# A graph attention kernel: seven new waits in front of the gathers of chunks 1 to 7

## The chip, the cores and the metric

The kernel runs on one core of one Trainium2 chip. The metric is the device time of one execution in microseconds (us). A comparison measures both kernels on the same chip.

## What is computed

6250 nodes carry 64 features each (x), and 200,000 edges, sorted by their receiver dst, carry two rows of 64 (edge_attr). Two layers follow each other, each with a residual and a layer norm:

```python
x = layernorm(x + L0(x, edge_attr, src, dst))
x = layernorm(x + L1(x, Wq, Wk, Wv, Wout, [src, dst]))
# L0: q = 0.95 * max(z)[src] * e1 + e0;  z_new = 0.2 z + 0.8 * segsum(q) / segsum(e1), where a node has edges
# L1: 4 heads; s = Q[dst] . K[src] / 8 per edge and head; softmax over the edges of a receiver;
#     out = x + mean over heads of (segsum(alpha * V[src])) @ Wout
```

## The kernel before, in words

Five engines run programs of their own and meet in semaphores: SP issues the plain DMAs, POOL (GpSimd) the gathers, PE (TensorE) multiplies, DVE (VectorE) and ACT (ScalarE) compute. P is 128, D is 64, UG is 13 (groups of four blocks of 128 nodes), S2 is 8, CPP is 4, NCH is 391.

**The edge stage** (0 to about 463 us in the profile) streams the edge rows through SBUF and sums them per receiver on PE. **The node stage** up to about 525 us folds the sums and normalises, 13 groups; POOL's `towards` and `normalise` (L551, L568) belong to it, and SP stores each finished group of x1 to DRAM (L433). When all 13 have landed (`s_x1d`, L579) POOL may begin to gather.

**The U stage** makes U, per node and head the row x1 @ (Wq Wk^T), turned. It has 13 steps. In step u PE turns the group's rows (`turn_nodes`, L1421) and multiplies them by A (`through_A`, L1437, which ends in `s_up`); then ACT copies one half of the two PSUM banks to U (`copy_U`, L287, called on L1172, signals `s_uc`) and DVE the other (L871, signals `s_ud`). ACT also keeps the turned rows of the next step (`keep_turned`, L1164). PE and ACT wait for all 13 `s_uc` and 12 `s_ud` before the attention starts.

**The attention stage** goes over 391 chunks of 512 edges. The edges' sender rows of x1 are gathered by POOL: four indirect DMAs per chunk, each 128 rows of 256 bytes, into one of eight slots of XS (`xs`, L269; the gather loop is L580 to L590, each gather adds 16 to `xg[k]`). The indices come from idx2, loaded by SP for a block of 8 chunks (`lx2`, three buffers). In step m of the pipeline PE turns the rows of chunk m (L1461, after `xg`), weighs the rows of chunk m-4 by its probabilities (L1471, `pv_done`), turns the probabilities of chunk m-3 (L1466) and forms the scores of chunk m-1 (L1513, `s_done`), in this order. DVE takes the maximum of chunk m-2 (L955) and updates the running sums l_st and O (L883, L886, `upd`), and masks. ACT exponentiates chunk m-2 (L1227), copies the turned rows to XT (L1193) and the columns of U to Ubuf (L1187, L1188, `u_done`), and copies turned probabilities (L1237). DVE adds 1 to `u_done` before the stage, 4 to `pv_done` and 2 to `s_done` (L821). So `u_done` is c-1 or more once ACT has done its part for chunk c-3.

The eight slots bound how far POOL may be ahead: before the gathers of chunk c (8 or more) it waits for `pv_done` c-3, which is the weighing of chunk c-8, and between the second and third of the four for `s_done` c-2. The first eight chunks have no such wait. A few chunks reach over more than one window of receivers and take an extra pass (`further_visits`).

**The output stage** scales O, multiplies by Wv and Wout, and normalises.

Of the kernel before, what the change touches and what calls it, by code (L numbers as in the profile page):

```python
# [22 lines left out]
def gnn_resnorm_kernel(nc, x, src, dst, edge, Wq, Wk, Wv, Wout, out):  # L23
# [30 lines left out]
    S2 = 8  # L54
# [11 lines left out]
    UG = -(-NB // 4)  # L66
# [5 lines left out]
    with ctx:  # L72
# [6 lines left out]
        def sem(name):  # L79
            return ctx.enter_context(nc.semaphore(name))  # L80
# [165 lines left out]
        s_eps, s_x1, s_x1d, s_xT, s_xTc, s_up, s_uc, s_ud = (  # L246
            sem(n) for n in ("eps_set", "x1_ready", "x1_stored", "xT_done", "xT_copied", "U_done", "U_copied", "U_copied_dve"))
# [21 lines left out]
        def xs(slot, c):  # L269
            return XS[:, (slot * CPP + c) * D:(slot * CPP + c + 1) * D]  # L270
# [187 lines left out]
        def _(pool):  # L458
# [121 lines left out]
            for c in range(NCH):  # L580
                b, k = c // S2, c % S2
                if k == 0:
                    pool.wait_ge(lx2[b % SB], 16 * (b // SB + 1) + (16 if b == NBL - 1 else 0))
                if c >= S2:
                    pool.wait_ge(pv_done, c - S2 + 5)
                for j in range(CPP):
                    if j == CPP // 2 and c >= S2:
                        pool.wait_ge(s_done, c - S2 + 6)
                    pool.indirect_dma_start(xs(k, j), None, x1_dram,  # L589
                                            bass.IndirectOffsetOnAxis(ap=idx2[b % SB][:, k * CPP + j:k * CPP + j + 1], axis=0)).then_inc(xg[k], 16)  # L590
# [995 lines left out]
```

## Time and profile before

| | us |
|---|---|
| timed runs, median of 3 | 2588.42 |
| lowest and highest | 2585.80, 2590.83 |
| span of the profiled execution | 2997.5 |

No time of its own beside the span is given for the profiled execution. It is one execution, recorded by the hardware profiler, and the timed runs are executions without the recorder. Times in the rows are microseconds from the first instruction; a mean is in nanoseconds where it says so. PE's ends are modelled, the starts are recorded. "Remote" is a wait whose release the profile doesn't attribute to an instruction of this core; "issue" is idle time in which nothing visible was waited for.

### The profile page before, as it was taken

How to read it: one execution, taken by the hardware profiler on the slowest of the kernel's cores; microseconds unless marked ns; L12 is line 12 of the kernel's file. 1: busy time of each engine (PE TensorE's matmuls, PEld its weight loads, DVE VectorE, ACT ScalarE, POOL GpSimd, SP SyncE). 2: the span in 40 equal slices, each digit the busy share in tenths (PEclk: the TensorE clock that was granted, in tenths of full speed). 3: DMA queues.
4: the chain of work that ended last, by engine and by line, in shares of the span. 5: the costliest groups of instructions: out<-in, count | busy, mean ns of one | idle time of the engine just before them, and what ended most of it. 6: DMA issues, size and time to landing. Idle time of an engine off the chain costs nothing.

```text
span 2997.5 us, 65526 instructions
## 1 busy us (share of the span) xinstructions
PE 2424.3 (81%) x18960; PEld 1749.1 (58%) x18961; DVE 1716.4 (57%) x5572; ACT 1313.2 (44%) x3792; POOL 1892.7 (63%) x2370
## 2 busy tenths in 40 slices
PE   4999998477888888887878788888888877778877
PEld 3888887254655555555555555555555555555555
DVE  8999997454545454444444444454544444444447
ACT  5555553443444344443444344443444343434434
POOL 3888887464666666666566566666666555656640
PEclk9999995665555555555555555555555555655558
DMA  6887772111111111111121111211112111112101
GB/s 177 257 255 254 254 252 51 21 31 33 32 38 32 39 38 33 38 32 37 30 38 31 36 35 36 38 32 39 37 33 39 29 36 30 37 29 39 31 18 24
DMA packets 178767, 194.85 MB, mean 65 GB/s; under 512 B 98339, under 2 KB 101235, under 8 KB 176481
## 3 DMA queue, kind: packets, MB, share of 16 engines
q1 hardware_dynamic: 128294, 138.91, 16.5%
q0 software_dynamic: 50048, 51.35, 9.1%
q8 instruction: 136, 2.23, 0.3%
q14 instruction: 289, 2.37, 0.3%
HBM read 184.87 MB, written 5.25 MB: 63 GB/s over the span
## 4 chain that ended last, share of the span: by engine, by line
another core or an unknown queue 30%; DVE 29%; issue 21%; DVEq 10%; PE 7%; ACT 1%; POOL 1%; ACTq 0%; DMA 0%; POOLq 0%; SPq 0%
DVE O L886 5%; DVE rmax L955 5%; DVE nm_old L968 4%; DVE l_st L883 3%; DVEq L982 2%; DVE big L723 2%; DVE cur L971 2%; DVEq L908 2%; DVE XT L877 1%; DVE nm_st L974 1%; DVEq L746 1%; DVEq L886 1%; PE psS L1513 1%; DVEq L904 1%
## 5 line engine op out<-in xcount | busy, mean ns | idle before, releaser
L589 POOL DMA_INDIRECT XS<-x_dram,dst_bs x1564 | 1482.4, 948 | 900.6 <-issue 419.9
L883 DVE SCALAR_TENSOR_TENSOR l_st<-l_st,alpha,rsum 64x1 f32 x782 | 168.2, 215 | 925.0 <-remote 891.3
L1471 PE MATMUL psVX<-XS,PmPT 128*128 128x64 f32 x1568 | 334.4, 385 | 243.6 <-ACT PmPT L1237 243.6
L1513 PE MATMUL psS<-XT,Ubuf 96*128 96x512 f32 x522 | 505.8, 1071 | 17.5 <-issue 6.2
L1471 PEld LDWEIGHTS psVX<-XS,PmPT 128*128 128x128 f32 x1568 | 308.8, 293 | 302.5 <-ACT PmPT L1237 302.2
L1237 ACT COPY PmPT<-psT 128x512 f32<-128x512 f32 x196 | 114.7, 585 | 760.1 <-remote 727.8
L1471 PE MATMUL psM<-XS,dst_bs 128*128 128x64 f32 x1560 | 343.2, 398 | 60.6 <-ACT dst_bs L1237 49.4
L1471 PEld LDWEIGHTS psM<-XS,dst_bs 128*128 128x128 f32 x1560 | 341.6, 321 | 71.0 <-ACT dst_bs L1237 58.3
L955 DVE TENSOR_REDUCE rmax<-psS 128x1 f32<-128x512 f32 x391 | 270.2, 691 | 34.2 <-remote 12.7
L1513 PE MATMUL psS<-dst_bs,Ubuf 96*128 96x512 f32 x260 | 250.3, 1065 | 7.1 <-ACT Ubuf L1188 1.6
L1466 PE MATMUL psT<-ident,dst_bs 128*128 128x128 f32 x780 | 207.6, 419 | 37.1 <-issue 34.2
L1227 ACT ACTIVATE dst_bs<-psS,cur 128x512 f32<-128x512 f32 x195 | 134.0, 687 | 234.0 <-DVE cur L971 216.6
L1461 PEld LDWEIGHTS psVX<-ident,XS 128*128 128x128 f32 x392 | 88.3, 226 | 220.8 <-issue 220.6
L1461 PEld LDWEIGHTS psN<-ident,XS 128*128 128x128 f32 x390 | 87.2, 224 | 216.6 <-issue 216.6
L1466 PE MATMUL psT<-ident,PmPT 128*128 128x128 f32 x784 | 203.7, 413 | 11.1 <-issue 7.1
L1227 ACT ACTIVATE PmPT<-psS,cur 128x512 f32<-128x512 f32 x196 | 134.7, 687 | 176.3 <-issue 99.0
L1237 ACT COPY dst_bs<-psT 128x512 f32<-128x512 f32 x195 | 114.1, 585 | 163.5 <-remote 130.5
L877 DVE TENSOR_SCALAR XT<-big,win_ids 32x512 f32<-32x512 f32 x269 | 129.3, 481 | 76.4 <-issue 76.0
L1466 PEld LDWEIGHTS psT<-ident,PmPT 128*128 128x128 f32 x784 | 162.5, 245 | 14.6 <-issue 8.8
L1466 PEld LDWEIGHTS psT<-ident,dst_bs 128*128 128x128 f32 x780 | 138.9, 216 | 54.5 <-issue 43.5
L1513 PEld LDWEIGHTS psS<-XT,Ubuf 96*128 96x128 f32 x522 | 135.1, 318 | 60.2 <-issue 60.1
L511 POOL TENSOR_TENSOR XS<-XS,zm 128x384 f32<-128x384 f32 x98 | 148.7, 1517 | 27.6 <-DVE zm L754 26.6
(281 smaller groups left out, 4133.2 us busy)
## 6 DMA issues: line engine op xcount, KB each, us to landing
big<-in_edge_attr_2x SPq DMA_DIRECT2D x342, 256.0 KB, 3.3
big<-dst_turned SPq DMA_DIRECT2D x49, 512.0 KB
XS<-x_dram,dst_bs POOLq DMA_INDIRECT x1564
O<-in_edge_attr_2x SPq DMA_DIRECT2D x48, 256.0 KB, 3.4
O<-codes_dram SPq DMA_DIRECT2D x200, 6.0 KB
x_dram<-x SPq DMA_DIRECT2D x12, 128.0 KB, 1.9
out<-big SPq DMA_DIRECT2D x12, 128.0 KB
codes_dram<-O SPq DMA_DIRECT2D x3, 384.0 KB
```

Source lines behind the costliest of these rows:

```text
L511: pool.tensor_tensor(buf[:, :, W:2 * W], buf[:, :, 0:W], zm[k // 2 % 2][:, :].unsqueeze(2).broadcast_to([P, 2 * SJ, W]), ALU.mult).then_in ...
L589: pool.indirect_dma_start(xs(k, j), None, x1_dram, bass.IndirectOffsetOnAxis(ap=idx2[b % SB][:, k * CPP + j:k * CPP + j + 1], axis=0)).the ...
L877: dve.tensor_scalar(t[D:96, :], dst_b[J // S2 % SB][:, J % S2 * CH:(J % S2 + 1) * CH], ids, None, ALU.not_equal).then_inc(s, 1)
L883: dve.scalar_tensor_tensor(out=ls, in0=ls, scalar=al[half], in1=rs[half], op0=ALU.mult, op1=ALU.add)
L886: last = dve.scalar_tensor_tensor(out=o, in0=o, scalar=al[half], in1=ps[half, :], op0=ALU.mult, op1=ALU.add)
L955: dve.tensor_reduce(rmax[:, q:q + 1], psSc[q][:, :], AX_X, ALU.max)
L1227: act.activation(Pms[a][:, :], psSc[a][:, :], ACT.Exp, bias=cur[:, a:a + 1], accum_out=rsum[:, a:a + 1]).then_inc(exp_done, 1)
L1237: act.copy(PTs[a][:, :], psT[:, :]).then_inc(pt_done, 1)
L1461: last = pe.transpose(psXc[b][:, j * P:(j + 1) * P], two, ident[:, :])
L1466: last = pe.transpose(ps[:, j * P:(j + 1) * P], probs[:, j * P:(j + 1) * P], ident[:, :])
L1471: last = pe.matmul(ps, pt[:, j * P:(j + 1) * P], xs(J % S2, j), start=(j == 0), stop=(j == CPP - 1))
L1513: pe.matmul(psSc[1 - a][:, :], Ubuf[1 - a][:, :], XT[(J - 1) % 3][:, :], start=True, stop=True).then_inc(s_done, 1)
```

## The change

In the gather loop POOL waits before the gathers of chunks 1 to 7. For chunk 1 it waits for `s_uc` 13 // 2 = 6, for chunk 2 for `s_uc` 13, for chunks 3 to 7 for `u_done` c-1, ACT's part of chunk c-3. Chunk 0 and the chunks from 8 on are as before.

```diff
                 b, k = c // S2, c % S2
                 if k == 0:
                     pool.wait_ge(lx2[b % SB], 16 * (b // SB + 1) + (16 if b == NBL - 1 else 0))
+                if c in (1, 2):
+                    pool.wait_ge(s_uc, UG * c // 2)
+                elif 2 < c < S2:
+                    pool.wait_ge(u_done, c - 1)
                 if c >= S2:
                     pool.wait_ge(pv_done, c - S2 + 5)
                 for j in range(CPP):
```

## Rows read from the trace of the kernel before

**Rows 1.** The head of the page.
```profile
span 2997.5 us, 65526 instructions
```

**Rows 2.** The page's costliest groups: busy, mean ns | idle before, releaser.
```profile
L589 POOL DMA_INDIRECT XS<-x_dram,dst_bs x1564 | 1482.4, 948 | 900.6 <-issue 419.9
```

**Rows 3.** Timeline of POOL, the first 33 gathers: start, us, instruction [idle before].
```profile
526.73 1.16 POOL L589 DMA_INDIRECT XS<-x_dram,dst_bs  x1 [2.24 <-DMA x_dram<-x]
...
531.95 0.94 POOL L589 DMA_INDIRECT XS<-x_dram,dst_bs  x1 [0.30 <-issue]
...
565.64 0.94 POOL L589 DMA_INDIRECT XS<-x_dram,dst_bs  x1 [0.30 <-issue]
593.72 1.14 POOL L589 DMA_INDIRECT XS<-x_dram,dst_bs  x1 [27.14 <-PE psVX L1471]
```

**Rows 4.** Timeline of ACT in the U stage, its copies to U.
```profile
525.87 1.50 ACT L287 COPY big<-psVX 64x256 f32<-64x256 f32 x4 [1.91 <-PE psM L1437]
...
533.88 1.50 ACT L287 COPY big<-psVX 64x256 f32<-64x256 f32 x4 [0.20 <-PE psM L1437]
...
541.69 1.50 ACT L287 COPY big<-psS 64x256 f32<-64x256 f32 x4 [4.60 <-remote]
...
560.62 1.50 ACT L287 COPY big<-psVX 64x256 f32<-64x256 f32 x4 [14.36 <-remote]
...
571.84 1.50 ACT L287 COPY big<-psS 64x256 f32<-64x256 f32 x4 [4.55 <-remote]
...
581.76 1.08 ACT L290 COPY big<-psVX 64x128 f32<-64x128 f32 x4
```

**Rows 5.** Waits from 526 to 584 us: who for whom, us in total, times, longest.
```profile
DVE big L287 <- remote: 32.8, 3, 17.2
ACT big L287 <- remote: 23.5, 3, 14.4
```

**Rows 6.** Timeline of PE: two steps of the U stage, then the first turned chunks.
```profile
533.73 0.48 PE L1437 MATMUL psS<-PmPT,A 64*128 64x256 f32 x1 [0.29 <-issue]
...
537.14 0.48 PE L1437 MATMUL psVX<-PmPT,A 64*128 64x256 f32 x1 [1.91 <-issue]
...
583.58 0.66 PE L1461 MATMUL psVX<-ident,XS 128*128 128x128 f32 x2 [2.48 <-ACT big L290]
584.03 0.63 PE L1461 MATMUL psN<-ident,XS 128*128 128x128 f32 x2
...
587.30 0.63 PE L1461 MATMUL psVX<-ident,XS 128*128 128x128 f32 x2
```

**Rows 7.** The edge stage: 0 to 400 us by windows, and waits from 50 to 455.
```profile
0.00:400.00 400.00, 334.07 (x9756) 296.69 (x9758) 384.39 (x739) 233.69 (x360) 307.65 (x609) 1.00 0.77 240
...
ACT XS L1117 <- PE psT L1327: 84.6, 49, 2.9
```

**Rows 8.** Waits from 900 to 1300 us.
```profile
DVE l_st L883 <- remote: 170.2, 34, 5.1
ACT PmPT L1237 <- remote: 162.5, 34, 4.9
```

**Rows 9.** Timeline of SP: loads of two successive blocks' indices.
```profile
933.89 0.37 SPq L407 DMA_DIRECT2D dst_bs<-in_src  x1
...
980.51 0.37 SPq L407 DMA_DIRECT2D dst_bs<-in_src  x1
```

**Rows 10.** Windows: 900 to 1300 us; the granted clock is the third last number.
```profile
900.00:1300.00 400.00, 337.38 (x1096) 228.56 (x1097) 195.67 (x760) 169.90 (x555) 259.80 (x275) 0.54 0.18 35
```

**Rows 11.** Timeline of PE: chunks turned while no gather goes out.
```profile
589.29 0.38 PE L1461 MATMUL psN<-ident,XS 128*128 128x128 f32 x2
...
591.75 0.38 PE L1461 MATMUL psVX<-ident,XS 128*128 128x128 f32 x2
...
594.50 0.38 PE L1461 MATMUL psN<-ident,XS 128*128 128x128 f32 x2
```

**Rows 12.** The last gather, and the line of the maxima (first and last start).
```profile
2906.55 0.94 POOL L589 DMA_INDIRECT XS<-x_dram,dst_bs  x1 [0.30 <-issue]
...
L955 DVE TENSOR_REDUCE rmax<-psS x391: 684/691/693, 587.5 to 2935.3; 128x1 f32<-128x512 f32 x196
```

**Rows 13.** Timeline of ACT: its last copy for chunk 0.
```profile
585.07 0.24 ACT L1188 COPY Ubuf<-big 64x64 f32 x1
```

**Rows 14.** The page's DMA issues: KB each, median us to landing.
```profile
x_dram<-x SPq DMA_DIRECT2D x12, 128.0 KB, 1.9
```

## The prediction

> **What bounds the kernel now.** I read the head of the page first: the profiled execution spans 2997.5 us [rows 1], 409.1 us more than the median of the timed runs, 2588.42. That gap matters more here than any row of the stage that is changed, so I keep two sums apart: one in the profiled execution's time, one in a timed run's.
>
> Next the costliest groups: 1564 gathers of 948 ns, with 419.9 us of idle time in front of them that waits for nothing [rows 2]. Between the start of the first and of the thirty-second gather lie 38.91 us in 31 steps [rows 3], so one gather costs POOL 1.255 us, the 0.30 us gap included, and a chunk of four 5.02 us. POOL cannot go faster than that through the 391 chunks.
>
> Then the U stage, on ScalarE's timeline. Its thirteen steps (one copy_U each) start at 525.87; the fifth starts at 533.88, a step per 2.00 us. Then come 541.69, 560.62 and 571.84, and the last, narrow one at 581.76, again (581.76-571.84)/5 = 1.98 us per step [rows 4]. Without the hole the stage would end at 525.87 + 12 x 2.00 + 1.08 = 550.95; it ends at 582.84. **The hole is 31.9 us**, and it ends when the first 32 gathers do (565.64 + 0.94) and what is queued has drained. The list of waits gives it to "remote" in 3 long waits of VectorE and 3 of ScalarE [rows 5], and TensorE's rows say why: the matmuls of the sixth step start at 533.73, but both readers get them at 541.69; those of the seventh start at 537.14 and are read at 560.62 [rows 4, 6]. So TensorE's completions come late, by up to 22 us, while gathers go out. In the edge stage, with plain DMAs at 240 GB/s and more and no gathers, the waits for TensorE average 84.6/49 = 1.7 us and none is remote [rows 7].
>
> In the attention the same thing recurs: over 400 us VectorE waits "remote" 34 times for 170.2 us, ScalarE 34 times for 162.5 [rows 8], about 5 us every second chunk. A block of 8 chunks takes 980.51-933.89 = 46.62 us, 5.83 a chunk [rows 9], at a granted clock of 0.54, between the two levels of 1.2 and 2.4 GHz [rows 10]. Where all gathers are in and none goes out, TensorE turns a chunk every 2.46 to 2.75 us [rows 11].
>
> **Which of this a timed run has.** Tail: from the last gather to the end the profile takes 2997.5-2906.55 = 91 us; at least 62.2 of them follow the last maximum at 2935.3 [rows 1, 12], and three chunk steps of 2.75 stand before it, so 70 to 91. With POOL never idle, a run takes 526.73 + 1563 x 1.255 = 2488.3, plus the tail, 2559 to 2579; the timed median leaves 9 to 30 for launch and end. With the hole of 31.9 us in the U stage, gather 33 starts at 593.72 as in the profile [rows 3], and the floor is 593.72 + 1531 x 1.255 = 2515.1 plus the tail, 2585 to 2606: the timed runs (2585.8 to 2590.8) leave between +3 and -18 us. And a timed attention stage cannot have 5.83 a chunk: (2588.4-551-62)/391 = 5.05 at most. That is POOL's 5.02. In a timed run the gathers thus go out nearly back to back for 1950 us, and TensorE delivers eleven fp32 matmuls (two turned tiles, four probabilities, four weighings, one score) per chunk beneath them. In the hole it delivered about forty in 38 us under the same pitch. The late completions must be mostly absent in a timed run, as if recording caused them. The edge stage may also be quicker when nothing is recorded, which would weaken this; hence the rivals.
>
> The SBUF page of the Trainium skill (SBUF: State Buffer, section "SBUF: two separate sides") states that engine ports and DMA ports are disjoint, so that a transfer and a computing engine don't slow each other. The profiled rows [rows 4, 5] look otherwise. By that rule alone the hole is no contention at the SBUF and the change only delays gathers, the forecast below; by the rows taken at face value it is the first rival.
>
> **The change part by part.** It removes and adds no transfer and no computation. It adds seven waits on POOL's queue, in front of chunks 1 to 7. Their own cost lies within the gap of 0.30 us ahead of a gather; nearest rows: chunk boundaries in the burst, where the gap stays 0.30 [rows 3]. I take 0, bound 0 to 7 x 0.3 = 2 us.
>
> Chunk 0 goes at 526.73 and POOL is through at 531.75. Chunk 1 waits for s_uc 6, the end of the sixth step's copy: 533.88 + 2.0 + 1.5 = 537.4, done 542.4. Chunk 2 waits for s_uc 13, the end of the U stage, 550.95. Chunks 3 to 7 wait for u_done of the chunk three before. ScalarE's copies for chunk 0 end 2.5 us after the stage does (585.31 against 582.84, by the rows of the attention's start, [rows 13]) and chunk 2's gathers alone take 5.02, so that wait is over; chunk c's data land some 2 us after its fourth gather (nearest row: 1.9 us for a store, [rows 14]) and are turned and copied in about 3 more, so u_done of chunk c-3 comes some 5 us ahead of POOL. Price 0; if each cost one step, 5 x 1 us.
>
> Queued behind the waits on POOL are all later gathers, and nothing else until the output stage. So POOL idles (537.4-531.75) + (550.95-542.4) = 14.2 us, and chunk 8's first gather is free to go at 550.95 + 24 x 1.255 = 581.1, where before it was at 565.64 + 1.255 = 566.9. Chunk 8 also waits for chunk 0's weighing. In the trace that comes 593.72-583.58 = 10.1 us after the first turned rows [rows 3, 6], so in a run without the hole at 551.7 + 10.1 = 561.8, before 566.9: no cover. After the change chunk 4 lands at 568 and that weighing follows by 570, ahead of 581.1. SP's loads of ids and of dst wait for upd and move with the chunks; they have tens of us of slack.
>
> Sum for a timed run: **+14.2 us**, 2588.4 + 14.2 = **2602.6**, since a POOL that never idles afterwards gives nothing back. For the profiled execution: hole gone, +581.1-593.7 = -12.6, and -8 if POOL is held to 5.83 a chunk from the start; if TensorE's start counts, up to -19. I expect a span of about 2983 there, shorter, while the timed run is longer.
>
> **The rivals.** (A) The hole is real in timed runs: U stage, chunk 8's gate. Let it be X us. Before, chunk 8 goes at the later of 566.9 and 561.8 + X; after, at 581.1. The gain begins to outweigh the loss at **X = 19.3**; at 31.9 it is 12.6 us: 2575.8. For it: the rows are plain, and the hole ends with the gathers. Against it: the floor above, and 5.05 a chunk.
> (B) The hole is there in part, X from 14 to 24.5, or the engines and not POOL pace a timed attention. In the latter case only the start slips: chunk 2 is turned at 551 + 5 + 2 = 558 where it was 551.7 + (587.30-583.58) = 555.4 [rows 6], about 3 us late: 2591. Against pacing by the engines: 2.46 to 2.75 us a chunk when fed [rows 11]. Either way within 0.2% (5.2 us, about what a measurement of this kernel can tell).
> (C) The change does not do what it says, because the counters are already past: s_uc counts ScalarE's steps from zero, u_done starts at 1, and the gathers start when only the first step is under way. I exclude it: it would need a U stage that is through before 531.75.
>
> **How the numbers follow.** Forecast (slower, 2602.6) 0.57; A and smaller gains 0.28; B 0.15. The likeliest case's own range is 2595 to 2606 (waits and steps priced, or X up to 10). The range over all must reach A: 2574 to 2606. Faster by over 0.2% 0.28, within it 0.15, slower 0.57.
>
> **What would show it.** In the profile after: gathers in groups, four from about 526.7, four from about 537, then from about 551 without a break; U-stage steps at 2.0 us throughout and no "remote" wait there; first turned rows of the attention near 552 instead of 583.58; chunk 8's first gather between 581 and 586; 5.83 a chunk later as before. If the hole stays though the gathers are spread, their burst is not its cause. If the timed run is faster by 8 us or more, the step that fails is "late completions are absent in a timed run". If it is unchanged, POOL was not what paces a timed attention.

## The result and the profile after

The changed kernel takes 2596.48 us in the median of 6 runs (2595.19 to 2602.54), the kernel before beside it 2589.62 (2585.80 to 2592.46). The ratio is 1.0034, 95% interval 1.0024 to 1.0045, or +8.8 us (6.2 to 11.7); the two medians lie 6.9 apart. Here and below a cost in us is the ratio less 1, times the median of the kernel before beside it. The change is a small loss. The prediction said +14.2 and slower.

The profile after spans 2600.8 us, its own time is 2602.54: 1.7 us lie around the span. Its head, its busy times, the chain that ended last by engine and by line, and the group of the gathers (busy, mean ns | idle before):

```profile
span 2600.8 us, 65526 instructions
PE 2078.3 (80%) x18960; PEld 1522.9 (59%) x18961; DVE 1722.9 (66%) x5572; ACT 1312.8 (50%) x3792; POOL 1905.7 (73%) x2370
...
POOL 47%; issue 24%; PE 12%; DVE 8%; DVEq 4%; DMA 4%; ACT 1%; ACTq 0%; POOLq 0%; SPq 0%
POOL XS L593 46%; DMA XS<-x_dram,dst_bs 3%; DVE big L727 2%; PE psS L1517 2%; PE psVX L1475 2%; DVEq L750 1%; PE psM L1475 1%; PE psT L1470 1%; PE psVX L1465 1%; DVEq L773 1%; DVE big L287 1%; DVE PmPT L753 1%; PE psA L1411 1%; PE psS L1411 1%; PE psA L1485 1%
...
L593 POOL DMA_INDIRECT XS<-x_dram,dst_bs x1564 | 1495.4, 956 | 497.5 <-issue 461.7
```

Most of the chain is the gathers' line: 46% of the span is POOL issuing them, and of the 24% "issue" the fixed gaps of 0.30 us in front of them (461.7 us in all, 18% of the span) are the larger part. Nothing is left of the 409 us by which the first profile of the kernel before [rows 1] was longer. Before any of it is put down to the change, that profile needs a second look (next section), since the timed runs moved the other way.

POOL's timeline after, around the new waits, at chunk 8's first gather (580.74), at the only later gap (chunk 31, a further visit), and the last gather:

```profile
528.12 1.16 POOL L593 DMA_INDIRECT XS<-x_dram,dst_bs  x1 [2.24 <-DMA x_dram<-x]
529.59 0.94 POOL L593 DMA_INDIRECT XS<-x_dram,dst_bs  x1 [0.31 <-issue]
...
538.84 0.94 POOL L593 DMA_INDIRECT XS<-x_dram,dst_bs  x1 [5.80 <-ACT big L287]
...
550.60 0.94 POOL L593 DMA_INDIRECT XS<-x_dram,dst_bs  x1 [7.08 <-ACT big L290]
...
555.60 0.94 POOL L593 DMA_INDIRECT XS<-x_dram,dst_bs  x1 [0.30 <-issue]
...
580.74 0.94 POOL L593 DMA_INDIRECT XS<-x_dram,dst_bs  x1 [0.30 <-issue]
...
705.27 0.94 POOL L593 DMA_INDIRECT XS<-x_dram,dst_bs  x1 [6.89 <-PE psS L1517]
...
2517.86 0.94 POOL L593 DMA_INDIRECT XS<-x_dram,dst_bs  x1 [0.31 <-issue]
```

The two waits on the U stage are there, released by ScalarE's copies. Less the fixed gap of 0.30 they are 5.50 and 6.78 us of idle time, 12.3 together. The waits on u_done (chunks 3 to 7) cost nothing: the gap stays 0.30, as at 555.60. From 580.74 to 2517.86 the 1531 steps average 1.265 us.

ScalarE in the U stage after, its copies to U:

```profile
527.26 1.50 ACT L287 COPY big<-psVX 64x256 f32<-64x256 f32 x4 [1.91 <-PE psM L1441]
529.89 1.50 ACT L287 COPY big<-psS 64x256 f32<-64x256 f32 x4 [0.73 <-PE psT L1441]
...
537.07 1.50 ACT L287 COPY big<-psS 64x256 f32<-64x256 f32 x4
538.87 1.50 ACT L287 COPY big<-psVX 64x256 f32<-64x256 f32 x4
...
549.26 1.08 ACT L290 COPY big<-psVX 64x128 f32<-64x128 f32 x4
```

No hole. The first step takes 2.63 us (527.26 to 529.89), those behind it 1.80 and the last 1.53, where the prediction took 2.00 for all of them.

### The profile page after: what moved, and what is told of

Same layout as the page of the kernel before. It is cut to its first block, busy times and chain, and to the rows that moved or that the text cites. A ratio compares the mean times of both kernels' runs of the same rounds, so it can differ in the third digit from the quotient of the medians.

```text
span 2600.8 us, 65526 instructions
## 1 busy us (share of the span) xinstructions
PE 2078.3 (80%) x18960; PEld 1522.9 (59%) x18961; DVE 1722.9 (66%) x5572; ACT 1312.8 (50%) x3792; POOL 1905.7 (73%) x2370
## 4 chain that ended last, share of the span: by engine, by line
POOL 47%; issue 24%; PE 12%; DVE 8%; DVEq 4%; DMA 4%; ACT 1%; ACTq 0%; POOLq 0%; SPq 0%
POOL XS L593 46%; DMA XS<-x_dram,dst_bs 3%; DVE big L727 2%; PE psS L1517 2%; PE psVX L1475 2%; DVEq L750 1%; PE psM L1475 1%; PE psT L1470 1%; PE psVX L1465 1%; DVEq L773 1%; DVE big L287 1%; DVE PmPT L753 1%; PE psA L1411 1%; PE psS L1411 1%; PE psA L1485 1%
## 5 line engine op out<-in xcount | busy, mean ns | idle before, releaser
L593 POOL DMA_INDIRECT XS<-x_dram,dst_bs x1564 | 1495.4, 956 | 497.5 <-issue 461.7
L1517 PE MATMUL psS<-XT,Ubuf 96*128 96x512 f32 x522 | 423.2, 907 | 15.8 <-ACT Ubuf L1192 15.7
L1465 PEld LDWEIGHTS psVX<-ident,XS 128*128 128x128 f32 x392 | 58.4, 185 | 395.7 <-issue 394.7
L1465 PEld LDWEIGHTS psN<-ident,XS 128*128 128x128 f32 x390 | 56.2, 182 | 394.6 <-issue 394.3
L1475 PE MATMUL psVX<-XS,PmPT 128*128 128x64 f32 x1568 | 285.8, 347 | 0.7 <-ACT PmPT L1241 0.7
L1475 PEld LDWEIGHTS psM<-XS,dst_bs 128*128 128x128 f32 x1560 | 282.6, 271 | 1.6 <-ACT dst_bs L1241 1.6
L1475 PE MATMUL psM<-XS,dst_bs 128*128 128x64 f32 x1560 | 282.6, 345 | 0.7 <-ACT dst_bs L1241 0.7
L1465 PE MATMUL psVX<-ident,XS 128*128 128x128 f32 x392 | 110.3, 377 | 169.1 <-DMA XS<-x_dram,dst_bs 165.7
L1465 PE MATMUL psN<-ident,XS 128*128 128x128 f32 x390 | 107.9, 371 | 166.5 <-DMA XS<-x_dram,dst_bs 165.2
L1517 PE MATMUL psS<-dst_bs,Ubuf 96*128 96x512 f32 x260 | 202.2, 872 | 7.1 <-ACT Ubuf L1192 7.1
L1470 PE MATMUL psT<-ident,dst_bs 128*128 128x128 f32 x780 | 171.4, 362 | 3.4 <-ACT dst_bs L1231 3.2
```

Of the source, the lines that this page charges most:

```text
L593: pool.indirect_dma_start(xs(k, j), None, x1_dram, bass.IndirectOffsetOnAxis(ap=idx2[b % SB][:, k * CPP + j:k * CPP + j + 1], axis=0)).the ...
L1465: last = pe.transpose(psXc[b][:, j * P:(j + 1) * P], two, ident[:, :])
L1470: last = pe.transpose(ps[:, j * P:(j + 1) * P], probs[:, j * P:(j + 1) * P], ident[:, :])
L1475: last = pe.matmul(ps, pt[:, j * P:(j + 1) * P], xs(J % S2, j), start=(j == 0), stop=(j == CPP - 1))
L1517: pe.matmul(psSc[1 - a][:, :], Ubuf[1 - a][:, :], XT[(J - 1) % 3][:, :], start=True, stop=True).then_inc(s_done, 1)
```

## The experiments

Ten runs follow, on three chips, each beside runs of the kernel before on its chip.

**The kernel before, profiled again.** No edit.

> The kernel before, unchanged, profiled once more. Theory P (late completions come with the one recorded execution, a timed run has none or few): a second profile of the same kernel can have a span near 2588, a U stage that ends near 551, and chunk 8's first gather at 566.9, POOL idle only there and at a few further visits; then the rest of the change's cost is given back somewhere else. Theory H (a part of the hole is in ordinary executions, X near 10 us): U stage ends near 561, chunk 8's first gather near 572. Theory R (the hole is a property of the kernel whenever it is recorded): span near 2997, 202 gaps over 0.35 us between gathers, as in the first profile.

Measured: 2589.64 us, span 2587.9. Head, chain, POOL's timeline at chunk 8's first gather, ScalarE's at the end of the U stage:

```profile
span 2587.9 us, 65526 instructions
...
POOL 47%; issue 24%; PE 11%; DVE 9%; DVEq 4%; DMA 3%; ACT 1%; ACTq 0%; POOLq 0%; SPq 0%
...
566.06 0.95 POOL L589 DMA_INDIRECT XS<-x_dram,dst_bs  x1 [0.31 <-issue]
567.32 0.95 POOL L589 DMA_INDIRECT XS<-x_dram,dst_bs  x1 [0.30 <-issue]
...
547.52 1.08 ACT L290 COPY big<-psVX 64x128 f32<-64x128 f32 x4
...
L589 POOL DMA_INDIRECT XS<-x_dram,dst_bs x1564: 942/947/1195, 526.8 to 2505.1; - x196
```

(The last line is the view by tile: ns min/median/max, first and last start.) The U stage ends at 547.52 + 1.08 = 548.6, where [rows 4] have 582.84, and the gather that had started at 593.72 [rows 3] starts at 567.32 without waiting: 33 gathers back to back from 526.75. In place of the "remote" waits of [rows 8], 900 to 1300 us has visible ones, and POOL waits for nothing but its fixed gap:

```profile
POOL XS L589 <- issue: 95.2, 312, 0.3
...
ACT dst_bs L1237 <- PE psT L1466: 82.1, 35, 4.5
ACT PmPT L1237 <- PE psT L1466: 73.4, 38, 3.8
DVE l_st L883 <- PE psVX L1471: 67.0, 35, 4.0
```

So the hole the change seems made to remove was in one recorded execution. Theory P (the late completions belong to that execution) holds; theory R (the hole is there whenever the kernel is recorded) falls, and theory H (a part of it in every execution) finds nothing in this profile; the run in which only chunk 1 waits tests it by the timed runs.

**A third profile of the kernel before.** No edit, on another chip.

> The kernel before, profiled a third time, on another chip. If late completions of TensorE come with the kernel, one in three profiles or more should show them again (span near 2997, over 200 gaps between gathers). If the first profile was one disturbed execution, this one is like the second: span 2585 to 2595, U stage without a hole, chunk 8's first gather 40.6 us after the first.

Measured: 2586.28 us, and the head and POOL's timeline:

```profile
span 2584.5 us, 65526 instructions
...
567.20 0.94 POOL L589 DMA_INDIRECT XS<-x_dram,dst_bs  x1 [0.30 <-issue]
```

567.20 against a first gather at 526.73: 40.5 us. Of the twelve profiles of this study one has the late completions. What disturbed that execution stays open.

**Only chunk 1 waits.**

```diff
-                if c in (1, 2):
-                    pool.wait_ge(s_uc, UG * c // 2)
-                elif 2 < c < S2:
-                    pool.wait_ge(u_done, c - 1)
+                if c == 1:
+                    pool.wait_ge(s_uc, 6)
```

> Only chunk 1 waits (s_uc 6); POOL idles once, about 5.5 us, then goes on back to back. Theory P: +5.5 us against the kernel before, the idle time passed on one to one. Theory H: the burst of 28 still goes out under the U stage, so the hole stays and hides the wait: 0 to +1 us.

Measured: ratio 1.0019 (1.0010 to 1.0028), +4.9 us (2.6 to 7.3). POOL's timeline:

```profile
539.07 0.94 POOL L591 DMA_INDIRECT XS<-x_dram,dst_bs  x1 [5.47 <-ACT big L287]
```

5.2 us of idle time cost 4.9. The first number is from the profile (5.47 less 0.30), the second from the timed runs. H said 0 to +1 and is out on them too.

**Chunk 1 waits for the whole U stage.**

```diff
-                if c in (1, 2):
-                    pool.wait_ge(s_uc, UG * c // 2)
+                if c == 1:
+                    pool.wait_ge(s_uc, UG)
```

> Chunk 1 waits for the end of the U stage (s_uc 13) and all later chunks follow it: POOL idles once for 17.5 us (533.0 to 550.6), 5 us more than in the changed kernel. Theory P: 17.3 us more than before if all is passed on, 5 us more than the changed kernel (which measured +6.9). Theory H: about 13 us more than before, since before loses some 4 to 5 us itself. Either way +5 against the changed kernel; if it is less, POOL's start does not pace the attention stage.

Measured: ratio 1.0061 (1.0047 to 1.0074), +15.8 us (12.2 to 19.2), by one gap:

```profile
550.87 0.94 POOL L593 DMA_INDIRECT XS<-x_dram,dst_bs  x1 [17.05 <-ACT big L290]
```

16.75 us of idle time.

**Only the waits on u_done.**

```diff
-                if c in (1, 2):
-                    pool.wait_ge(s_uc, UG * c // 2)
-                elif 2 < c < S2:
+                if 2 < c < S2:
                     pool.wait_ge(u_done, c - 1)
```

> Chunks 1 and 2 go out at once, chunk 3 waits for ScalarE's part of chunk 0 (about 552.9 in the time of the changed kernel's profile): POOL idles 9.8 us instead of 12.3. Theory P: 2.5 us less than the changed kernel, +9.8 at most against before. Theory H: twelve gathers are a burst of 15 us, long enough for a small hole at the end of the U stage: +4 to +7 against before.

Measured: ratio 1.0035 (1.0023 to 1.0047), +9.1 us (6.0 to 12.2):

```profile
552.35 0.94 POOL L591 DMA_INDIRECT XS<-x_dram,dst_bs  x1 [10.39 <-ACT Ubuf L1190]
```

10.1 us of idle time. Twelve gathers went out back to back, and the U stage's steps are 1.80 us from the third on all the same. The intervals overlap that of the changed kernel, so "2.5 us less" is not shown. It also shows that the waits on u_done are free only because chunk 2's wait stands in front of them.

**The changed kernel again.** No edit.

> The changed kernel, unchanged, on another chip than the first time, beside the same runs of the kernel before as the next three. Theory P (POOL's idle time is passed on one to one): its profile idles 12.3 us, so about +12 us. If it is again +7 to +9, part of the idle time is given back, and more than in the kernels with one gap.

Measured: ratio 1.0054 (1.0040 to 1.0068), +14.0 us (10.3 to 17.6). The same two gaps:

```profile
529.08 1.16 POOL L593 DMA_INDIRECT XS<-x_dram,dst_bs  x1 [2.24 <-DMA x_dram<-x]
...
539.82 0.94 POOL L593 DMA_INDIRECT XS<-x_dram,dst_bs  x1 [5.83 <-ACT big L287]
...
551.60 0.94 POOL L593 DMA_INDIRECT XS<-x_dram,dst_bs  x1 [7.09 <-ACT big L290]
```

12.3 us again. One comparison gave 8.8, the other 14.0, and the idle time lies between them, just above the first interval and inside the second. That a part is given back is not shown. Profile against profile nothing is given back: the first profile of the changed kernel is 12.9 us longer than the second of the kernel before, 1.4 of them ahead of the first gather, 11.4 from the first gather to the last and 0.1 behind it. That profiled execution was also the slowest of the six (2602.54); where the other five were quicker no profile shows.

**The attention starts late, the gathers don't.** The kernel before with extra copies in the last 5 steps of the U stage, then in all 13 (`UG - 13` for `UG - 5`). They write to places that are unused there.

```diff
                 act.wait_ge(s_up, u + 1)
+                if u >= UG - 5:
+                    for t in ((PmX[:, :], dst_bs[:, 0:CH].bitcast(F32)), (Pms[1], PTs[1]))[u % 2]:
+                        act.copy(t, u_banks[u % 2][0][:, :])
                 copy_U(act.copy, u, 0).then_inc(s_uc, 1)
```

> The kernel before; ScalarE makes two extra copies of 128x512 (0.585 us each) to unused places in each of the last 5 steps of the U stage, so the attention starts some 5.9 us late while all gathers go out as before. By the second profile of the kernel before, TensorE's weighings and scores are 5.6 to 8.6 us ahead of the gathers that wait for them. Theory P: 0 to +1 us. Theory S (the start of the attention paces the end): +5.9.

> The same extra copies in all 13 steps, some 15.2 us. Theory P: only what exceeds the lead of 5.6 us counts, +9.6, and it shows as idle time of POOL at chunks 8 to 13. Theory S: +15.2.

Measured for 5 steps: ratio 1.0005 (0.9996 to 1.0014), +1.3 us (-1.0 to 3.6); from its first gather (526.54) to the end of the U stage it took 26.6 us, 4.8 more than the 21.8 of the second profile of before. For 13 steps: 1.0026 (1.0016 to 1.0037), +6.7 us (4.1 to 9.6), with the U stage 12.1 us longer (529.06 to 562.98), less than the 15.2 I had reckoned. POOL's timeline in the second, at chunks 8, 9 and 12 (chunks 10 and 11 have a gap of 0.58 each):

```profile
573.87 1.13 POOL L589 DMA_INDIRECT XS<-x_dram,dst_bs  x1 [4.74 <-PE psVX L1474]
...
581.87 0.94 POOL L589 DMA_INDIRECT XS<-x_dram,dst_bs  x1 [0.57 <-PE psS L1516]
...
598.38 1.18 POOL L589 DMA_INDIRECT XS<-x_dram,dst_bs  x1 [0.81 <-PE psS L1516]
```

An attention that starts 4.8 us late costs nothing that can be told from zero, 12.1 us late it costs about the idle time that it makes on POOL: 4.44 us at chunk 8 and 1.34 at chunks 9 to 12, 5.8 together. Theory S (the start of the attention paces the end: +5.9 and +15.2, or 4.8 and 12.1 by the stretches measured) falls. The weighing that chunk 8 waits for thus has a lead of 12.1 - 4.44, about 8 us. It covers an attention that starts late. Waits in front of the gathers themselves, which is what the change adds, it does not cover.

**The idle time in the middle.**

```diff
-                    pool.wait_ge(pv_done, c - S2 + 5)
+                    pool.wait_ge(pv_done, c if c in (100, 200, 300) else c - S2 + 5)
```

> The kernel before; only chunks 100, 200 and 300 wait for a later weighing (pv_done c instead of c-3), so that POOL stands still three times some 4 to 7 us in the middle of the stage, and the U stage is untouched. Theory P: the time grows by the sum of these gaps, 12 to 20 us, as at the start. If gaps in the middle cost less than their length, something else paces the stage there.

Measured: ratio 1.0078 (1.0064 to 1.0092), +20.2 us (16.6 to 23.8). The three gaps:

```profile
1042.26 0.94 POOL L589 DMA_INDIRECT XS<-x_dram,dst_bs  x1 [4.22 <-PE psM L1471]
...
1549.66 0.94 POOL L589 DMA_INDIRECT XS<-x_dram,dst_bs  x1 [3.62 <-PE psM L1471]
...
2060.42 0.94 POOL L589 DMA_INDIRECT XS<-x_dram,dst_bs  x1 [8.31 <-PE psM L1471]
```

15.25 us in the one profile. No less than the idle time is lost, so POOL paces the middle of the stage as well. The profiled execution itself took 2603.20, 15.7 us above the median before and close to its own 15.25; three of the other four took 2607.73 to 2610.49. The gaps differ from 3.6 to 8.3 us, and whether those executions had longer ones, or something adds to them, is open.

**A shorter node stage, to gain on both kernels.** The kernel before, where ScalarE's Square also sums (one activation of 64 columns per block) and VectorE's reduction goes.

```diff
-                    act.activation(sq1[(g - 2) % 2][:, 0:nb * D], x1[:, b0 * D:(b0 + nb) * D], ACT.Square).then_inc(g_sq, 1)
+                    for b in range(nb):
+                        last = act.activation(sq1[(g - 2) % 2][:, b * D:(b + 1) * D], x1[:, (b0 + b) * D:(b0 + b + 1) * D], ACT.Square,
+                                              accum_out=stat[:, b0 + b:b0 + b + 1])
+                    last.then_inc(g_sq, 1)
...
-                dve.tensor_reduce(s_, sq1[g % 2][:, 0:nb * D].rearrange("p (b d) -> p b d", d=D), AX_X, ALU.add).then_inc(g_var, 1)
```

> The kernel before with a shorter stage ahead of the first gather: in the node stage ScalarE sums the squares itself (one activation with its sum per block) and VectorE's reduction of them (0.41 us in each of 13 steps of 3.95 us that VectorE fills) is left out. Theory P (POOL never idles after its first gather): what the first gather comes earlier is gained at the end, one to one, some 4 to 5 us: the first gather near 522 and the time 0.2% lower. If the node stage doesn't get shorter, POOL (3.3 us a step) or ScalarE (about 3.0) sets it and nothing changes. If the gather comes earlier and the time stays, theory P is wrong about the start.

Measured: ratio 1.0004 (0.9995 to 1.0013), no change. POOL's first gather, and TensorE's folding of the sums in the same profile:

```profile
526.53 1.16 POOL L589 DMA_INDIRECT XS<-x_dram,dst_bs  x1 [2.23 <-DMA x_dram<-x]
...
474.66 0.77 PE L1402 MATMUL psA<-ident,big 128*128 128x128 f32 x2
...
475.65 0.77 PE L1402 MATMUL psA<-ident,big 128*128 128x128 f32 x2
```

And the windows of 475 to 515 us, first of the kernel before (second profile), then of this one. Busy us stand in the order TensorE, its weight loads, VectorE, ScalarE, POOL, and the granted clock is the third last number:

```profile
475.00:515.00 40.00, 40.00 (x244) 40.00 (x245) 36.24 (x68) 13.62 (x40) 31.01 (x58) 0.50 0.14 31
...
475.00:515.00 40.00, 40.00 (x244) 40.00 (x244) 33.45 (x59) 19.49 (x104) 30.87 (x59) 0.50 0.14 32
```

The gather does not come earlier. TensorE folds a block every 0.985 us without a gap, 3.94 us for a group of four, and is busy for 40.00 of 40 us in both kernels, at a granted clock of 0.50 (the level of 1.2 GHz). The step of 3.95 us is TensorE's; VectorE, at 36.24 us nearly as long, only looked like its owner, and what the edit took from it (2.8 us) changed nothing. Since the first gather did not move, this says nothing about theory P. No kernel here beats the one before.

## Why the prediction was right, and where not

Idle time of POOL that a kernel adds (from its profile, less 0.30 per gap) and what it costs in timed runs:

| kernel | first gather at, us | idle, us | cost, us (95% interval) |
|---|---|---|---|
| attention late, 5 steps | 526.5 | 0 | 1.3 (-1.0 to 3.6) |
| attention late, 13 steps | 529.1 | 5.8 | 6.7 (4.1 to 9.6) |
| chunk 1 only | 528.7 | 5.2 | 4.9 (2.6 to 7.3) |
| u_done only | 527.0 | 10.1 | 9.1 (6.0 to 12.2) |
| the change, two comparisons | 528.1, 529.1 | 12.3 | 8.8 (6.2 to 11.7), 14.0 (10.3 to 17.6) |
| in the middle | 528.7 | 15.25 | 20.2 (16.6 to 23.8) |
| all after the U stage | 528.9 | 16.75 | 15.8 (12.2 to 19.2) |

The kernel before has its first gather at 526.73 to 526.75 in its three profiles. Further visits (chunk 31) are left out of the idle time: that one gap is 4.6 to 6.9 us long in the eleven undisturbed profiles, which alone makes two profiles differ by up to 2.3 us.

- **"A POOL that never idles afterwards gives nothing back"**: right within what the runs can tell. The cost follows the idle time within the intervals, but for two that miss it by 0.6 and 1.4 us. One thing runs beside it: in six of the profiles, none of them of the kernel before, the first gather comes 1.4 to 2.4 us later. The delay begins in the edge stage, which no edit touches (the same matmuls start at 461.90 in the second profile of before and at 463.32 in the first of after). If the timed runs have it too, the cost in the middle is inside its interval and that of the first comparison of the change further outside. Whether it belongs to those kernels or to chance was not tried.
- **+14.2 us of idle time**: the mechanism was right, the size was off by 1.9; it is 12.3. The mis-sized term is the step of the U stage. The 2.00 us were a mean over the first four steps, and these hold the long first one (2.32) and a disturbed fourth (2.10); the two between took 1.80 in that profile too:

```profile
528.19 1.50 ACT L287 COPY big<-psS 64x256 f32<-64x256 f32 x4 [0.42 <-PE psT L1437]
529.98 1.50 ACT L287 COPY big<-psVX 64x256 f32<-64x256 f32 x4
531.78 1.50 ACT L287 COPY big<-psS 64x256 f32<-64x256 f32 x4
```

  From the first copy to the last the profile after has 22.0 us (527.26 to 549.26) where the prediction had 24.0, and the second wait is 6.78 us in place of 8.55. The forecast of 2602.6 us lies 6.1 above the measured 2596.48. The 1.9 us explain a part; the distance from 12.3 us of idle time to a cost of 8.8 no run explains, and the repetition gave 14.0.
- **Chunk 8 free at 566.9 before and 581.1 after**: 567.32 and 580.74 in the profiles. The second agrees in part by luck: the first gather was 1.4 us later in that profile, and counted from it chunk 8 goes at 52.6, not at the 54.4 forecast.
- **Waits on u_done and the waits' own cost, 0**: right. A gather's data land 2.5 us after its issue (median of the profile after), where I had taken 2 from a store.
- **Late completions absent in a timed run**: right. "As if recording caused them" is wrong: eleven recorded executions of these kernels are without them. It was one execution, and my forecast of a span near 2983 for the profile after, made as though any profile would have them, missed by 382 us. The same mistake made the sign "5.83 a chunk later" wrong (5.06 measured).
- **The floor**: POOL's step was too short and the rest too long. The second profile of before gives (2505.1-526.8)/1563 = 1.266 us a gather, not 1.255, since some gathers take longer (up to 1.195 us where the median is 0.947; why is open) and chunk 31 waits once; the tail is 82.8 us; launch and end take 1.7, where I had left 9 to 30. The sum 526.75 + 1563 x 1.266 + 82.8 + 1.7 is 2590, as it must be, since its terms are those of that execution (2589.64). With these values the floor with a hole would have been 593.72 + 1531 x 1.266 + 82.8 + 1.7 = 2616, 25 us above every timed run then known. So the argument against rival A was stronger than the prediction knew, and its 0.28 too much.
- **The rule of the Trainium skill's SBUF page** (SBUF: State Buffer, "SBUF: two separate sides"), that transfers and computing engines don't slow each other: the traces agree with it. From its third step on the U stage keeps 1.80 us a step beside 4, 8 or 12 gathers and beside an unbroken row of them, and ScalarE's copies take 1.50 us in each case. Whatever made TensorE late in the first profile is not the ordinary effect of the gathers.

## What to carry to other kernels

When the profiled execution is far longer than the timed runs, take what the timed runs can hold (the pacing queue's step times its count, plus head and tail) and ask of each stall whether it fits, before a change is aimed at it; better still, profile again. An engine that issues back to back for the whole of a stage turns the waits put in front of its instructions into time, here about one to one and at the start of the stage as in the middle. In a stage where two engines look equally long, check whose instructions have no gap before you shorten one.

## What the runs showed of the hardware

- In one recorded execution of twelve, and in one of three with the same program, TensorE's completions came up to 22 us late while gathers went out, and a chunk took 5.83 us in place of 5.06. The cause was not found. A low clock did not begin it: the matmuls of the U stage were still recorded with 0.38 us each at 537.69, as in the second profile, when those started at 533.73 were already overdue (ScalarE had waited for them since 537.1 and read them at 541.69; in the second profile it reads them 1.6 us after their start), and with 0.59 and 0.63 only from 537.90 on.
- The first gather starts from 526.5 to 529.1 us, and late in kernels with nothing changed ahead of it too (528.68 and 528.73 in two of them). The three profiles of the kernel before agree within 0.02 us. Runs of one kernel on one chip lie up to 9.4 us apart (2586.55 to 2595.95 in sixteen), so single runs are unfit for a difference of 10 us.
- The granted clock in the attention was 0.54 in the disturbed execution [rows 10] and 0.62 and 0.70 over the same 400 us in the second profile of before and the profile after, between the levels 1.2 and 2.4 GHz. Between these two the time did not follow it: POOL's step is 1.25 us in the median of both.
